# Four causal taps of a depthwise convolution: from VectorE's multiply-adds to TensorE's diagonal matrices, in five of eight scan stages

## The reference

```
xin   = in_proj_w @ ctx                               # 512 channels x 512 positions
xc    = depthwise causal conv of xin, 4 taps, + conv_b  # xc[l] = b + sum_j w[j] * xin[l-3+j]
u     = silu(xc)
dt_lo, B, C = x_proj_w @ u                            # 16, 16, 16 rows
delta = softplus(dt_proj_w @ dt_lo + dt_proj_b)
state[n] = state[n] * exp(delta * A[n]) + delta * u * B[n]     # along positions, 16 states n
y     = sum over n of state[n] * C[n]  +  D * u
x     = x + tanh(g_xattn) * (y * silu(layernorm(x))).T
```

## Time and profile before

| | us |
|---|---|
| median of 3 runs | 1687.87 |
| lowest, highest | 1685.1, 1689.21 |
| profiled execution | 1696.96 |
| its span | 1695.2 |
| VectorE busy | 1498.9 (88%) |
| TensorE busy | 1259.6 (74%) |
| ScalarE busy | 823.0 (49%) |
| GpSimd busy | 874.9 (52%) |

### The profile page before, as it was taken

One profiled execution on the slowest core, in us unless ns is written; L12 is line 12 of the kernel. 1 busy time (PEld: TensorE's weight loads), 2 busy tenths in 40 slices (PEclk: granted clock), 3 DMA queues, 4 the chain that ended last, 5 costly groups with the idle time before them and its releaser, 6 DMA issues.

```text
span 1695.2 us, 13647 instructions
## 1 busy us (share of the span) xinstructions
PE 1259.6 (74%) x4084; PEld 694.2 (41%) x4084; DVE 1498.9 (88%) x1511; ACT 823.0 (49%) x1288; POOL 874.9 (52%) x449
## 2 busy tenths in 40 slices
PE   5566576677666876778777998789987899805678
PEld 2122132333233322334343656556665566603344
DVE  3999999899989999999987999899998999967883
ACT  4455537363725363532692666546665444404341
POOL 0357636643663367433245456764557666466521
PEclk7798789789978898898887999989999899956888
DMA  6244435523542354334155777766886788654421
GB/s 224 74 135 124 108 99 143 131 67 107 143 132 60 90 142 115 89 94 125 38 137 137 227 250 265 250 218 214 262 251 205 269 274 265 222 162 122 138 74 50
DMA packets 99834, 264.26 MB, mean 156 GB/s; under 512 B 10832, under 2 KB 11344, under 8 KB 93616
## 3 DMA queue, kind: packets, MB, share of 16 engines
q1 hardware_dynamic: 87936, 225.36, 44.3%
q0 software_dynamic: 11440, 37.50, 6.5%
q10 hardware_dynamic: 384, 0.52, 0.1%
HBM read 233.73 MB, written 29.62 MB: 155 GB/s over the span
## 4 chain that ended last, share of the span: by engine, by line
DVE 22%; PE 18%; issue 8%; DMA 5%; POOL 4%; ACT 4%; SPq 0%; DVEq 0%; ACTq 0%; POOLq 0%
PE banks L1054 8%; DVE state L1506 7%; DVE banks L1498 5%; PE banks L1065 3%; DMA expert_w<-in_moe_w 3%; POOL state L433 2%; DMA ys_d<-expert_out 2%; PE banks L1195 2%; DVE y_scan L1517 2%; DVE x_res L1680 1%; PE banks L1033 1%; DVE du L1265 1%; DVE small L1299 1%; PE banks L974 1%; PE banks L1225 1%
## 5 line engine op out<-in xcount | busy, mean ns | idle before, releaser
L433 POOL TENSOR_TENSOR state<-state,bc_rows 128x1024 f32<-128x1024 f32 x256 | 605.7, 2367 | 673.2 <-DVE banks L1498 673.1
L974 PE MATMUL banks<-state,ident 128*128 128x512 f32 x640 | 366.5, 706 | 194.2 <-POOL state L433 193.9
L1506 DVE TENSOR_TENSOR_SCAN state<-decay,banks 128x1024 f32<-128x1024 f32 x176 | 402.1, 2285 | 9.8 <-ACT decay L658 5.1
L1498 DVE TENSOR_TENSOR banks<-du,bc_rows 128x1024 f32<-128x1024 f32 x256 | 351.6, 1374 | 22.2 <-PE banks L974 8.2
L1054 PE MATMUL banks<-z_gate,expert_w 128*128 128x256 f32 (+1 forms) x1504 | 288.8, 351 | 12.0 <-DMA expert_w<-in_moe_w 6.7
L974 PEld LDWEIGHTS banks<-state,ident 128*128 128x128 f32 x640 | 127.1, 215 | 405.4 <-POOL state L433 289.9
L658 ACT ACTIVATE decay<-delta,neg_a 128x511 f32<-128x511 f32 x352 | 231.2, 713 | 104.8 <-DVE state L1506 51.8
L1054 PEld LDWEIGHTS banks<-z_gate,expert_w 128*128 128x128 f32 x1504 | 252.5, 193 | 67.2 <-issue 25.5
L1506 DVE TENSOR_TENSOR_SCAN state<-expert_w,banks 128x1024 f32<-128x1024 f32 x80 | 182.9, 2286 | 2.8
L1065 PE MATMUL banks<-expert_w,hidden 128*128 128x512 f32 x316 | 159.0, 619 | 2.9 <-DVE hidden L1527 2.9
L1517 DVE TENSOR_TENSOR y_scan<-y_scan,state 128x1024 f32<-128x1024 f32 x96 | 136.2, 1420 | 11.5 <-POOL state L433 11.5
(11 more groups left out here) (233 smaller groups left out, 1670.8 us busy)
## 6 DMA issues: line engine op xcount, KB each, us to landing
bc_rows<-bc_d SPq DMA_DIRECT2D x208, 512.0 KB, 4.9
expert_w<-in_moe_w SPq DMA_DIRECT2D x48, 1536.0 KB, 9.1
ys_d<-expert_out SPq DMA_DIRECT2D x32, 512.0 KB, 10.3
ctx_t<-in_ctxT SPq DMA_DIRECT2D x8, 512.0 KB, 6.7
x_res<-in_x SPq DMA_DIRECT2D x4, 1024.0 KB, 10.5
xn_d<-y_scan SPq DMA_DIRECT2D x4, 1024.0 KB, 7.5
ys_d<-expert_out SPq DMA_DIRECT2D x15, 256.0 KB, 9.2
out_x<-x_res SPq DMA_DIRECT2D x3, 1024.0 KB, 4.3
```

The costliest lines, as they stand in the source:

```text
L433: nc.gpsimd.tensor_tensor(W[:, c % 4], W[:, c % 4], bcast2(BC[:, u, 1, :]), ALU.mult).then_inc(mulc_done, 1)
L974: mm = nc.tensor.matmul(PS[:, m], ID[:, :], W[:, c % 4, m, :], start=False, stop=True, skip_group_check=True)
L1498: nc.vector.tensor_tensor(drive(s), DU[:, s % 2, 2 * h:2 * h + 2, :], bcast2(BC[:, u, 0, :]), ALU.mult).then_inc(mulb_done, 1)
L1506: nc.vector.tensor_tensor_scan(flat(W[:, c % 4]), flat(DAS[c % da_slots(s, i)]), flat(drive(s)), 0.0, ALU.mult, ALU.add).then_inc(scan_don ...
```

## The change

For the preparation of stages 1 to 5, VectorE's 12 multiply-adds a stage are gone. ScalarE makes 12 diagonal matrices of 128 x 128 for a layer (identity times one tap's weights, `make_taps`), and for each tile, besides the first tap into `du`, a plain copy of xin into `delta`. TensorE then makes the sum in the tile's own bank: the identity times `du`, and three diagonals times the copy, shifted by 1 to 3 positions. ScalarE takes silu straight from the bank, tile by tile. The waits that told TensorE that a bank may be overwritten (`conv_step`) are now on that silu (`u_ready`). In the lists TensorE has `conv` of tiles 0 and 1 and `in_proj(p, 1)` ahead of the wait for `yg_done` from stage 1 on, and `conv` of tiles 2 and 3 behind `sum_state` of units 5 and 6.

```diff
+        TAPS = [flat(YSB[:, :, :])[:, i * P:(i + 1) * P] for i in range(RT * D // P)]
+        TAPS += [FREE[:, 2 * P + i * P:3 * P + i * P] for i in range(ET * (DC - 1) - len(TAPS))]
...
             def conv_tap_one(s, et):
...
-                nc.scalar.activation(DU[:, s % 2, et, :], pre_bank(s, et), ACT.Identity, bias=CH[:, lay(s), et, C_CB:C_CB + 1],
-                                     scale=CH[:, lay(s), et, DC - 1:DC]).then_inc(tap_first, 1)
+                tap = nc.scalar.activation(DU[:, s % 2, et, :], pre_bank(s, et), ACT.Identity, bias=CH[:, lay(s), et, C_CB:C_CB + 1],
+                                           scale=CH[:, lay(s), et, DC - 1:DC])
+                if 1 <= s <= FIRST_B:
+
+                    tap = nc.scalar.activation(DEL[:, s % 2, et, :], pre_bank(s, et), ACT.Copy)
+                tap.then_inc(tap_first, 1)
+
+            def make_taps(layer):
+                if layer:
+                    act.wait_ge(conv_done, ET * (NB - 1))
+                for et in range(ET):
+                    for j in range(DC - 1):
+                        ins = nc.scalar.activation(TAPS[et * (DC - 1) + j], ID[:, :], ACT.Copy, scale=CH[:, layer, et, j:j + 1])
+                ins.then_inc(taps_ready, 1)
+
+            def silu_pair(s, pair):
+                for et in (2 * pair, 2 * pair + 1):
+                    act.wait_ge(conv_done, ET * (s - 1) + et + 1)
+                    nc.scalar.activation(DU[:, s % 2, et, :], pre_bank(s, et), ACT.Silu).then_inc(u_ready, 1)
...
             for pair in range(2):
                 conv_tap(0, pair)
+            act.wait_ge(masks, 6)
+            make_taps(0)
             conv_silu(0)
...
                     if c == 3 and f >= 0:
                         z_gate(f)
+                        silu_pair(p, 0)
+                    if c == 5 and f < 0:
+                        silu_pair(p, 0)
                     if c == 6:
                         conv_tap(p, 1)
                 if s == NB:
                     break
-                conv_silu(p)
+                silu_pair(p, 1)
...
+                        if s == NB - 2 and i == 2 and c == 6:
+                            make_taps(1)
...
+            def conv(s, et):
+
+                pe.wait_ge(taps_ready, lay(s) + 1)
+                pe.wait_ge(tap_first, ET * s + et + 1)
+                bank = pre_bank(s, et)
+                nc.tensor.matmul(bank, ID[:, :], DU[:, s % 2, et, :], start=True, stop=True)
+                for j in range(DC - 1):
+                    sh = DC - 1 - j
+                    mm = nc.tensor.matmul(bank[:, sh:], TAPS[et * (DC - 1) + j], DEL[:, s % 2, et, 0:L - sh],
+                                          start=False, stop=True, skip_group_check=True)
+                mm.then_inc(conv_done, 1)
+
             def x_proj(s):
+                if s:
+
+                    pe.wait_ge(u_ready, ET * s + 3)
                 x_some(s, range(ET))
...
                 if f >= 0:
+                    conv(p, 0)
+                    conv(p, 1)
+                    in_proj(p, 1)
                     pe.wait_ge(yg_done, f + 1)
                 sum_skip(s, 0)
                 for c in range(HPT):
                     sum_state(s, 0, c)
+                    if f < 0 and c in (1, 2):
+                        conv(p, c - 1)
...
-                    if c == 3:
+                    if c == 3 and f < 0:
                         in_proj(p, 1)
+                    if c in (5, 6):
+                        conv(p, c - 3)
                     if c == 5 and g >= 0:
...
-                        conv(p, 0)
                     if c == 2 and g >= 0:
                         shared_hidden(g, 1)
...
-                    if c == 6:
-                        conv(p, 1)
```

More of the change, by code:

```diff
@@ L180, in build @@
         inproj_done, tap_first, conv_step, u_ready = sem("inproj_done"), sem("tap_first"), sem("conv_step"), sem("u_ready")
+        taps_ready, conv_done = sem("taps_ready"), sem("conv_done")
         xproj_done, xdbl_ready, dt_done, dt_read = sem("xproj_done"), sem("xdbl_ready"), sem("dt_done"), sem("dt_read")
@@ L237, in rows_in, with convs @@
             return 16 * sum(BLOCKS[i] for i in range(j % 2, j + 1, 2))
+        def convs(s):
+            return 3 * ET * (s - FIRST_B) if s else 0
         def lay(s):
@@ L537, in conv_tap_one @@
                 act.wait_ge(inproj_done, ET * s + et + 1)
-                nc.scalar.activation(DU[:, s % 2, et, :], pre_bank(s, et), ACT.Identity, bias=CH[:, lay(s), et, C_CB:C_CB + 1],
-                                     scale=CH[:, lay(s), et, DC - 1:DC]).then_inc(tap_first, 1)
+                tap = nc.scalar.activation(DU[:, s % 2, et, :], pre_bank(s, et), ACT.Identity, bias=CH[:, lay(s), et, C_CB:C_CB + 1],
[14 more added lines that the diff above has]
+                    nc.scalar.activation(DU[:, s % 2, et, :], pre_bank(s, et), ACT.Silu).then_inc(u_ready, 1)
             def conv_silu(s):
-                act.wait_ge(conv_step, 3 * ET * (s + 1))
+                act.wait_ge(conv_step, convs(s) + 3 * ET)
                 nc.scalar.activation(flat(DU[:, s % 2]), flat(DU[:, s % 2]), ACT.Silu).then_inc(u_ready, ET)
             def silu_one(s, et):
-                act.wait_ge(conv_step, 3 * ET * s + 3 * (et + 1))
+                act.wait_ge(conv_step, convs(s) + 3 * (et + 1))
                 nc.scalar.activation(DU[:, s % 2, et, :], DU[:, s % 2, et, :], ACT.Silu).then_inc(u_ready, 1)
@@ L916, in in_proj @@
                     if pair and s:
-                        pe.wait_ge(conv_step, 3 * ET * s + 4 + et - 1)
+                        pe.wait_ge(u_ready, ET * s + et - 1)
                     for k in range(KC):
@@ L927, in in_one @@
                 if et >= 2:
-                    pe.wait_ge(conv_step, 3 * ET * s + 3 * (et - 1))
+                    pe.wait_ge(conv_step, convs(s) + 3 * (et - 1))
                 for k in range(KC):
@@ L1177, in tile_turn @@
                         if n == 5:
-                            pe.wait_ge(conv_step, 3 * ET * p + 3 * (ET - 1))
+                            pe.wait_ge(conv_step, convs(p) + 3 * (ET - 1))
                             x_some(p, (0, 1))
@@ L1263, in conv_one @@
                     else:
-                        dve.wait_ge(conv_step, 3 * ET * s + 3 * et + m)
+                        dve.wait_ge(conv_step, convs(s) + 3 * et + m)
                     nc.vector.scalar_tensor_tensor(
@@ L1462, in slots @@
                 at = lambda v: v.rearrange("p (k t) -> p k t", k=TOPK)
-                link(nc.vector.tensor_scalar(at(NROW1), slk, 1.0 / P, -0.5 + 0.5 / P, ALU.mult, ALU.add))
+                link(nc.vector.tensor_scalar(at(NROW1), slk, 1.0 / P, 0.5 + 0.5 / P, ALU.mult, ALU.add))
                 link(nc.vector.tensor_scalar(CHUNK1, NROW1, float(1 << 23), -float(1 << 23), ALU.add, ALU.add))
@@ L1466, in slots @@
                                                     op1=ALU.subtract))
-                nc.vector.tensor_scalar(CHUNK1, CHUNK1, 1.0, None, ALU.add)
-                link(nc.vector.tensor_scalar(NROW1, NROW1, -1.0, None, ALU.add))
+                link(nc.vector.tensor_scalar(NROW1, NROW1, -float(P + 1), None, ALU.add))
                 ends = T1[:, 0:(NTILE) * NE].rearrange("p (j e) -> p j e", e=NE)
```

## The result

| | before | after |
|---|---|---|
| median, us | 1688.54 (4 runs, 1685.1 to 1693.21) | 1746.04 (4 runs, 1740.7 to 1747.46) |
| span of the profiled execution | 1695.2 | 1744.1 |
| VectorE busy | 1498.9 | 1459.4 |
| TensorE busy | 1259.6 | 1325.0 |

The changed kernel takes 1.032 times as long (95% interval 1.0286 to 1.0355): 57.5 us by the medians. The prediction was 1740 in a range of 1715 to 1764. The profiled execution of before was a long one of its kind (1696.96 us), so the two spans differ by 48.9 us only; what follows counts positions in the profiled executions, where VectorE's first instruction of stage 5's preparation of delta (L1276, now L1330) starts at 933.47 us instead of 878.32, 55.2 us later.

A forecast was written before the change was run, and what follows sets the result against it. VectorE's list was taken to bound stages 0 to 4. Losses of 1.6, 4.9, twice 17.4 and 11.0 sum to 52.3 us: 1749.3 on the profiled execution, 1740 after allowing 9.1 for the median; range 1715 to 1764.

The forecast's parts named there:

- stage 0, unit 8: Stage 0's scan of unit 8 starts 1.6 us later, behind TensorE's added tiles and `in_proj`, then silu, load and decay.
- stage 1, unit 4; unit 8: Stage 1: scan of unit 4 wins 1.4 us as groups fill TensorE's idleness; with the 6.3 lost at unit 8, 4.9 lost.
- stage 4, both terms: Stage 4: 7.7 us lost at unit 4 plus 3.3 at VectorE's second `shared_add`, waiting for the shared pair: 11.0.
- rival A: TensorE's added work is off the path, so all 44.3 us of VectorE's time is won: 1643.6 us; chance 0.05.
- The head: Start of stages 2 to 4: three TensorE groups, 10.3 us, delay `sum_skip` and unit 4's buffer; scan 7.7 us later.
- The tail: End of turn 0, stages 0 to 3: unit 8's decay waits behind tile 3's silu; 9.7 us lost, 6.3 in stages 0, 1.
- Rival B: Only the start of stages loses; the decay of unit 8 does not come last: no change, 1686 us; chance 0.05.
- Rival C: TensorE's low clock: a tile takes up to 6.40 us instead of 3.44; 1764 us, or 1789 if all slow; chance 0.12.
- What was priced at nothing: ScalarE's 20 copies of 0.78 us and its diagonals were claimed to hide in ScalarE's waits, costing nothing.

The follow-up runs named there:

- e7: Changed kernel with the moves of e1 and e2, and the shared expert's second pair behind `sum_state` of unit 4: 1658.8 us, 0.9816 times the kernel before.
- e1: Changed kernel with convolution of tiles 0 and 1 and `in_proj` of tiles 2 and 3 ahead of the shared expert's first pair on TensorE: 1710.7 us.
- e4: Changed kernel with the identity matmul of tiles 0 and 1 written three times in the preparation of stages 3 to 5: 1754.5 us.
- e5: Changed kernel without the three diagonal matmuls, so a tile is one matmul; copies and list order stay: 1705.4 us.
- e2: Changed kernel with ScalarE's silu of tiles 2 and 3 moved from ahead of the decay of unit 8 to behind that of unit 10: 1712.6 us.
- e6: Kernel before the change plus ScalarE's copies and 24 diagonals, which nobody reads, VectorE's convolution kept: 1693.0 us against 1692.0.

## Why the prediction was right

Its terms against positions in the two traces (each is how much later the named scan starts, less what the stage started late):

| | predicted | measured |
|---|---|---|
| stage 0, unit 8 | 1.6 | 3.2 |
| stage 1, unit 4; unit 8 | -1.4; 4.9 | -1.6; 5.2 |
| stages 2 and 3, unit 4 | 7.7 each | 7.0, 7.4 |
| stages 2 and 3, tail | 9.7 each | 9.1, 9.1 |
| stage 4, both terms | 11.0 | 10.1 |
| router's scores, stages 1 to 3 | 0 | 3.1, -2.2, 3.0 |
| sum | 52.3 | 55.2 with 0.2 ahead of stage 0 |

The terms of the prediction sum to 52.3 and measured 51.1: stage 0 was 1.6 too small, tails, heads and stage 4 together some 3 too large. That these nearly cancel is luck, though no term but stage 0's was off by more than 1 us. The 3.9 us of the router's scores were in no term. The signs that it had named are there: 11.0 to 11.9 us of wait at unit 4 of stages 2 to 4, released by `sum_state`; the scan of unit 8 behind a decay, and ScalarE before it waiting for tile 3 (7.98 us in stage 2, 4.54 in stage 0); unit 4 of stage 1 earlier.

**The bound.** Right: VectorE's list set the end, and 39.5 us less in it with the new waits made a longer kernel. The removed work was mis-sized in one place: 60 x 0.738 = 44.3 counts the overlap of neighbours twice (six of them took 4.02 us in the earlier trace rows, not 4.43), and the busy time fell by 39.5. The sum used 4.0 for each of ten pieces, which is the right 40; rival A's 1643.6 should have been 1648. Its condition, the work off the path, is nearly met in e7: 1658.8.

**The head.** The mechanism is shown by e1 (the work out of that place: the waits go) and by e4 and e5 (more or less work in it: they grow or shrink). 10.3 us for three groups were 10.28. The decay of unit 4 was not last, as said; it ended some 3.6 us before the buffer was free, predicted 3.8. The 7.7 came out as 7.0 and 7.4.

**The tail.** Shown by e2: only ScalarE's order changed, 33.4 of an expected 34 us came back. Rival B, that the decay of unit 8 is not last, falls with it. From the end of the scan of unit 6 to the scan of unit 8 stage 2 took 19.0 us, predicted 19.7: tile 2 was over in 3.43 where 4.2 had been taken. The rest was worth what the prediction had taken: silu 0.60, and 1.30 from the table load to the next instruction. The drain of some 1380 ns that the Trainium skill ("ScalarE: Activation LUTs", What ACT_TABLE_LOAD costs) adds to each load, and by which, in the estimate of the prediction, the tails would have lost 5.5 us less, is not in this trace either, on neither side of the load: the silu of 401.56 ends at 402.16, the load starts at 402.17, the next instruction at 403.47.

**Stage 0** was the term off by most of its size. The sum took 1.75 for each `sum_state`, and that of unit 1 had been 1.98 in the earlier trace rows; it took 3.75 here, at a granted clock of 0.50 from 64.7 to 68.3 us (the lower level), and moved all behind it by 1.8:

```profile
64.73 3.75 PE L1021 MATMUL banks<-state,ident 128*128 128x512 f32 x4 [0.93 <-POOL state L441]
68.31 1.04 PE L971 MATMUL banks<-du,ident 128*128 128x512 f32 x2
```

The lists of stage 0 are the same in e1 and e4, and there it took 1.98 and VectorE's wait at unit 6 was 1.7 instead of 3.5 us, so this comes and goes between executions. The waits at units 6 and 7 (3.47 and 0.73), for decays behind the silu of tiles 0 and 1, were not in the prediction; they cost nothing here, since the decay of unit 8 came later still.

**Stage 1's head** as said: the groups filled the idle time up to the gating, and `sum_skip` took 1.98 us instead of 3.60.

**Rival C.** Nothing of it at the heads of stages 2 to 4: every group took 3.43 us, and the granted clock was 1.00 from 394.5 to 404.8 us, the upper level. At the head of stage 1, behind a slow `sum_state` (3.78), the first group took 4.13, as the prediction had it. In the tails the `sum_state` ahead of the convolution was slow (3.46 in stage 2, 3.78 in stage 1 at a granted clock of 0.50), and in stage 1 the start of tile 2 too (4.28 for the group).

**What was priced at nothing** on ScalarE was worth at most a few us (e6). The router's scores, of which the sum says nothing, were worth 3.9.

Open: the medians differ by 57.5 us, the positions at stage 5 by 55.2, the spans by 48.9. Part of it is given back behind stage 5 in these two executions. I did not test whether the tiles' stages gain, or only vary.

## What to carry to other kernels

Where one engine's list sets the end, work taken out of it is won only as far as its new place lies in an idle time of the other engine, or ahead of nothing that the first one waits for; read that from the new engine's timeline, at the item which stands behind the new work, not from its busy share. An idle time in front of an item belongs to what is listed ahead of that item. Put a consumer that waits (here a silu) behind whatever on its engine could run already: the same instructions in three other places turned 57 us of loss into 31 of gain.

## What the runs showed of the hardware

The wait of VectorE for the router's scores was between 2.3 and 7.3 us in every kernel, and by no pattern of the edits. It goes with TensorE's clock: the 32 instructions of the router's products took 6.85 us in stage 1 and 4.13 in stage 2 of the changed kernel.

```profile
342.83 6.85 PE L1047 MATMUL banks<-router_w,y_scan 128*128 128x16 f32 x32
...
531.53 4.13 PE L1047 MATMUL banks<-router_w,y_scan 128*128 128x16 f32 x32
```

From 341 to 350 us the granted clock was 0.50, its lower level; from 528 to 536 it was 0.78 on the mean. In the 27 places of the nine traces the products took either 3.6 to 4.1 us, and VectorE then waited 2.3 to 4.1, or 6.85, and it waited 5.9 to 7.3. The three places of an execution came to between 10.8 and 17.5 us, and the runs of one kernel spread over 4 to 11 us, so differences of a few us between two profiles are read at the places of the edit, and not from the spans.
